# Expert stages of a four-layer kernel: half of the low-part subtractions on another engine

## The reference

```
x = x + attn_i(layernorm(x))
x = x + ffn_i(layernorm(x))
```

```
ffn0: 64 experts of 64 hidden features, best 8: silu(x Wg) * (x Wu) * weight, then Wd; and one shared expert
ffn1: 8 experts of 128, best 2:                 relu(x W1)^2 * weight, then W2
ffn2: 4 experts of 512:                         relu(x W1 + b1) * weight, then W2, + b2
ffn3: 8 experts of 128:                         silu(x Wg) * (x Wu) * weight, then Wd
```

## Time and profile before

| what | value |
|---|---|
| three runs | 2252.23, 2265.64, 2268.24 us (median 2265.64) |
| the profiled execution: span from first to last instruction | 2272.5 us |
| PE matmul busy | 1805.3 us (79%) |
| DVE busy | 1404.8 us (62%) |
| ACT busy | 1006.3 us (44%) |
| POOL busy | 899.5 us (40%) |
| mean granted TensorE clock, share of full speed | 0.834 |

### The profile page before, as it was taken

How to read it: one execution, slowest core, us unless ns; L and a number is a source line. 1 busy time by engine, 2 the same in 40 slices (tenths; PEclk the granted TensorE clock), 3 DMA queues, 4 the chain that set the end, 5 groups by cost and what they waited for, 6 DMA issues and landing times. The chain is left out here.

```text
span 2272.5 us, 28698 instructions
## 1 busy us (share of the span) xinstructions
PE 1805.3 (79%) x8124; PEld 1409.1 (62%) x8124; DVE 1404.8 (62%) x3292; ACT 1006.3 (44%) x1863; POOL 899.5 (40%) x819
## 2 busy tenths in 40 slices
PE   6899986799999999994777577677699984442799
PEld 6899986577777777762555355455366653221587
DVE  5532146676666666654566477667566658887566
ACT  3421014454455545542555355435277752222454
POOL 3723001355555555550000055400178853221355
PEclk9996576899999999995666588889799986666799
DMA  5001001765445545531000055210011110000455
GB/s 72 1 10 12 1 1 40 159 141 114 106 111 117 117 108 108 116 81 33 1 1 1 18 117 107 57 36 1 20 38 37 44 38 1 1 1 1 93 119 121
DMA packets 122543, 130.52 MB, mean 57 GB/s; under 512 B 48582, under 2 KB 67274, under 8 KB 122474
## 3 DMA queue, kind: packets, MB, share of 16 engines
q1 hardware_dynamic: 112328, 128.72, 26.1%
q10 hardware_dynamic: 10146, 0.94, 0.5%
HBM read 126.09 MB, written 3.54 MB: 57 GB/s over the span
## 5 line engine op out<-in xcount | busy, mean ns | idle before, releaser
L787 POOL TENSOR_TENSOR ffn_alo<-ffn_a,ffn_ahi 128x512 fp32r<-128x512 f32 x520 | 670.6, 1292 | 509.2 <-ACT ffn_ahi L748 505.4
L814 DVE TENSOR_TENSOR ffn_a<-ffn_G,ffn_mask 128x512 f32<-128x512 f32 x384 | 264.7, 689 | 241.8 <-ACT ffn_G L756 218.3
L756 ACT ACTIVATE ffn_G<-ffn_G 128x512 f32<-128x512 f32 x384 | 223.5, 582 | 357.6 <-PE ffn_G L117 355.4
L748 ACT ACTIVATE ffn_ahi<-ffn_a 128x512 fp32r<-128x512 f32 x520 | 324.6, 624 | 35.8 <-DVE ffn_a L818 31.8
L115 PE MATMUL ypsum<-ffn_ahi,ffn_hi 128*128 128x512 f32 x520 | 227.7, 438 | 52.6 <-POOL ffn_alo L787 37.1
L115 PE MATMUL ffn_G<-xn_hi,ffn_hi 128*128 (+1 forms) x520 | 220.4, 424 | 29.9 <-DVE ffn_lo L794 26.8
L818 DVE TENSOR_TENSOR ffn_a<-ffn_U,ffn_a 128x512 f32<-128x512 f32 x320 | 221.4, 692 | 29.7 <-DVE ffn_a L814 0.5
L116 PE MATMUL ffn_G<-xn_lo,ffn_hi 128*128 (+1 forms) x520 | 214.2, 412 | 0.0
L117 PE MATMUL ffn_G<-xn_hi,ffn_lo 128*128 (+1 forms) x520 | 214.0, 412 | 0.0
L116 PE MATMUL ypsum<-ffn_alo,ffn_hi 128*128 128x512 f32 x520 | 210.0, 404 | 0.0
L117 PE MATMUL ypsum<-ffn_ahi,ffn_lo 128*128 128x512 f32 x520 | 208.6, 401 | 0.0
(11 more groups left out here) (567 smaller groups left out, 3657.6 us busy)
## 6 DMA issues: line engine op xcount, KB each, us to landing
ffn_mask<-mask_rows_top SPq DMA_DIRECT2D x128, 512.0 KB, 6.9
ffn_mask<-mask_rows_top SPq DMA_DIRECT2D x16, 1024.0 KB, 8.5
ffn_mask<-mask_rows_zone SPq DMA_DIRECT2D x16, 1024.0 KB, 8.4
ffn_mask<-mask_rows_steps SPq DMA_DIRECT2D x16, 512.0 KB, 4.9
x<-in_L_attn_x SPq DMA_DIRECT2D x8, 256.0 KB, 5.6
ffn_raw<-in_L_ffn_expert_gate_k SPq DMA_DIRECT2D x16, 128.0 KB, 3.8
ffn_raw<-in_L_ffn_expert_up_k SPq DMA_DIRECT2D x16, 128.0 KB, 3.8
ffn_raw<-in_L_ffn_expert_down_k SPq DMA_DIRECT2D x16, 128.0 KB, 3.8
```

The costliest lines, as they stand in the source:

```text
L748: act.activation(ahi[i][:, :], a[i][:, :], ACT.Copy).then_inc(k.ahi_done, 1)
L756: act.activation(gate if masked(c) else a[c % RING_A][:, :], gate, how, **kw).then_inc(k.r_done, 1)
L787: eng.tensor_tensor(alo[i][:, :], a[i][:, :], ahi[i][:, :].bitcast(F32), ALU.subtract).then_inc(k.alo_done, 1)
L814: dve.tensor_tensor(out, gate[:, :], mask(c), ALU.mult).then_inc(k.t_done, 1)
```

## The change

Low parts of odd chunks move to DVE and count on a new semaphore, `alo_odd`. Those of even chunks stay on GpSimd and count on `alo_done`. DVE computes the low part of an odd chunk c - 1 right behind `scale(g, c)`. Whoever waited for `alo_done` (PE before `down`, DVE and ScalarE before they overwrite a buffer of the ring) now waits for the semaphore of that chunk's parity, at a count of its own. In all, 256 low parts go to DVE (16 + 4 + 8 + 4 chunks of 8 groups) and 264 stay on GpSimd.

```
+    k.alo_odd = k.sem("alo_odd")
+    k.alo_even0 = k.alo_odd0 = 0
...
+        evens, odds = (C + 1) // 2, C // 2
+        even0, odd0 = k.alo_even0, k.alo_odd0
+
+        def wait_rest(eng, g, c):
+            if c % 2:
+                eng.wait_ge(k.alo_odd, odd0 + g * odds + c // 2 + 1)
+            else:
+                eng.wait_ge(k.alo_done, even0 + g * evens + c // 2 + 1)
+
+        def wait_rest_before(eng, g, c):
+            wait_rest(eng, *((g, c - RING_A) if c >= RING_A else (g - 1, C + c - RING_A)))
...
                 def down(g, c):
                     pe.wait_ge(k.ahi_done, at(g, c) + 1)
-                    pe.wait_ge(k.alo_done, at(g, c) + 1)
+                    wait_rest(pe, g, c)
...
                     if not masked(c) and exists(g, c, RING_A):
-                        act.wait_ge(k.alo_done, at(g, c) - RING_A + 1)
+                        wait_rest_before(act, g, c)
...
-            def rest(eng, g, c):
+            def rest(eng, g, c, done):
                 i = c % RING_A
                 eng.wait_ge(k.ahi_done, at(g, c) + 1)
-                eng.tensor_tensor(alo[i][:, :], a[i][:, :], ahi[i][:, :].bitcast(F32), ALU.subtract).then_inc(k.alo_done, 1)
+                eng.tensor_tensor(alo[i][:, :], a[i][:, :], ahi[i][:, :].bitcast(F32), ALU.subtract).then_inc(done, 1)
+
+            def rest_vector(dve, g, c):
+                if c % 2:
+                    rest(dve, g, c, k.alo_odd)
+
+            def rest_gpsimd(pool, g, c):
+                if c % 2 == 0:
+                    rest(pool, g, c, k.alo_done)
...
                     if exists(g, c, RING_A):
-                        dve.wait_ge(k.alo_done, at(g, c) - RING_A + 1)
+                        wait_rest_before(dve, g, c)
...
                         post(vector_step, dve, g, c)
                         scale(g, c)
+                        behind(lambda g, c: rest_vector(dve, g, c), g, c, 1)
...
                 def finish():
+                    rest_vector(dve, GROUPS - 1, C - 1)
...
-                        behind(lambda g, c: rest(pool, g, c), g, c, 1)
+                        behind(lambda g, c: rest_gpsimd(pool, g, c), g, c, 1)
                 def finish():
-                    rest(pool, GROUPS - 1, C - 1)
+                    rest_gpsimd(pool, GROUPS - 1, C - 1)
```

More of the change, by code:

```diff
@@ L890, in moe_stage @@
     k.chunk0 += GROUPS * C
+    k.alo_even0 += GROUPS * ((C + 1) // 2)
+    k.alo_odd0 += GROUPS * (C // 2)
     k.up0 += GROUPS * C if gated else 0
```

## The result

The change makes the kernel slower: 2291.59 us (median of 4 runs, 2285.55 to 2296.88) against 2263.07, a ratio of 1.0143 (95% interval 1.0115 to 1.0170). A later set of runs gave 1.0127 (1.0093 to 1.0161). The forecast was 2285, between 2252 and 2316, with 0.37 for "slower by more than 1%" and 0.56 for "within 1%": the time lies in the range, the sign is right, and the likelier class was the wrong one, by less than half a percent.

What follows compares the result with a forecast made beforehand. The matmul engine (PE) was taken as busiest, with DVE setting ffn1's pace. Terms 21 + 2 + 2 - 5 - 0.6 = +19.4 us, carried over to the runs' median of 2265.64, gave 2285 us, range 2252 to 2316.

Steps and rivals of the forecast that it cites:

- The odd low part in ffn0: ffn0, odd chunks: DVE starts it 0.60 us behind the second multiply, takes 0.69, PE's weight load follows 0.11 later.
- 0.20 us later: ffn0, odd downs: PE's weight load comes at 706.12 against 705.92 now, 0.20 us later.
- the new semaphore counts: On the sequencers: they cost only register instructions that run ahead of the engines, so nothing.
- A pair at 4.51: ffn0: gate starts of a pair of chunks lie near 4.51 us apart instead of 4.315.
- +21 and +2 for ffn0: ffn0: 8 groups x 14 odd chunks x 0.19 us gives +21 us; group 0's weight split adds +2.
- the wait of once a group: ffn0, chunk 11: POOL waits for DVE's moments ahead of low(10), PE idles 2.27 us; it stays as now.
- The +2 for group 0: ffn0, group 0: weight split loads DVE to 2.3 us a chunk against PE's 2.16; 5 us at most, taken as +2.
- The loss is nearly all at odd downs.: ffn0 before the change: 0.10 us lost a pair of chunks, nearly all at the down matmuls of odd chunks.
- ffn1, +2: ffn1: added DVE subtractions against xn's first piece getting 0.87 us faster, +0.15 a group, +2 us with uncovered ones.
- ffn2, -5: ffn2: two of three low parts queued behind rstd leave POOL, -5 us, between -13 and +2.
- The port as a rival: DVE's subtraction often sits behind POOL's, 0.33 to 0.87 us a hit; ffn0 +37 on top, 2322 us; chance 0.18.
- The class: Whole program against a 1% (23 us) bound: slower by more 0.37, within 1% 0.56, faster by more 0.07.

Runs made afterwards that it cites:

- the kernel with the part between the multiplies: Against the change: DVE computes the odd low part between the next chunk's two multiplies, not behind both; ratio 1.0015 to the kernel before, ffn0 610.3 us.
- the kernel with spare subtractions: Against the kernel before, low parts all on GpSimd: DVE adds an unawaited two-SBUF-input subtraction at each odd chunk's place of the change; ratio 1.0294.

## Why the prediction was right, point by point

- **The odd low part in ffn0.** Forecast: start 0.60 behind the second multiply, 0.69 long, at PE 0.11 after that. Measured: 0.60, 0.68, 0.06. The mechanism and the place are shown by the kernel with the part between the multiplies.
- **0.20 us later.** It is 0.30: against the start of the last up matmul, odd low parts end at +0.11 us in the kernel before and at +0.41 in the change (medians of chunks 25 to 29, groups 2 to 7). The missing 0.1 is nearly all in a term that the forecast put at nothing, the new semaphore counts: the register instruction behind the wait holds both multiplies back. No run has the new counts with the low parts left in their places, so what this alone costs is not measured.
- **A pair at 4.51.** Measured 4.55 in clean pairs and 4.57 in the mean. Of the 0.30 us, 0.26 reach the pair: the weight load had been 0.21 late for a matmul less than 0.1 late, so part of the delay had cover. Chunks with a norm step in front lose 0.1 more (2.53 to 2.56 us against 2.44).
- **+21 and +2 for ffn0** (+22.5, +21.9). Right in sum, and that is luck in part. Groups 1 to 6 are 3.2 us longer each: 14 odd chunks at 0.28 in the mean are 4.0, and 0.8 come back, most of it at the wait of once a group, whose three chunks take 9.3 us and not 9.75. The forecast had 14 x 0.19 = 2.7 and nothing back. Of the 0.45 at the wait, about half is that the clock fell in 3 groups and not in 4. The +2 for group 0 did not show: from its first high part to group 1's first gate it is as long as before in one pair of profiles and 1 us shorter in the other.
- **"The loss is nearly all at odd downs."** True of groups 1 to 7, wrong as a statement on parity; it led to the missed gain of the kernel with the parts between.
- **ffn1, +2** (+2.5 in both pairs of profiles). xn's first piece fell from 1206 to 342 ns as forecast, and the stage did not get shorter. Two other profiles with ffn1 split as in the change have 157 us, so +2.5 is the low end.
- **ffn2, -5** (-2.9). The 6.6 us went; 6.8 us of weight loader waiting for xn came, and 8.8 of short waits for POOL's even parts are there. The term was sized without what is late next.
- **The port as a rival**, 0.18: it did not decide, but it is there, seven times in ffn0 of the change and at some 200 of 253 places in the kernel with spare subtractions. I had no case in the trace of before in which POOL was the blocked one.
- **The class.** 0.56 stood on "within 1%" with a sum of +19.4 against a bound of 23. With the sum that near the bound the two chances should have been nearly even.

## What to carry to other kernels

A subtraction that takes 1.29 us on one engine and 0.68 on another is not faster there if it has to stand behind two instructions: ask at which microsecond its result is wanted, and put it in the order by that. Freed time on an engine that hardly ever ended a wait is worth next to nothing. A count that is worked out behind another wait delays what stands behind both, so new semaphore counts are a term of the sum too. And look for short waits that repeat at a fixed place of each group; here one number of a hand-written order took as much out of ffn0 as moving half of the work had put in.

## What the runs showed of the hardware that I had not expected

- Two engines' SBUF reads hold each other up in both directions: DVE's subtraction up to 1825 ns for 682, POOL's up to 1839 for 1293, and a program of 2260 us loses 67 us by some 250 such instructions, of which the same number with one SBUF input cost 7.
- PE idle for 2.0 to 2.5 us found its clock at half in 2 to 6 groups of 7 and at full in the others, at the same place in the code, and lost about 1.5 us more where it was at half.
- A register instruction of 40 ns between an awaited semaphore and DVE's next instruction goes with a start 0.09 us later: 121 ns behind the activation's end, for 32.
